# Last stage: first rounding of the convolution's result on GpSimd, ahead of its split of the recurrent state, instead of on ScalarE

## The reference, cut to what matters

```
# layer 1: LSTM over t, then a feed-forward with quantised activations
h = bit_linear(lstm_h, w1)          # act_quant(x): scale = 127 / max|x| per row,
h = depthwise_conv1d(h, conv_w, b)  #   clip(round(x * scale), -128, 127) / scale
h = silu(h)                         # 128 sequences x 512 channels for each step
x = x + bit_linear(h, w2)           # act_quant(h) again: this is the rounding moved here
# layer 2: h2 = tanh(h2 @ Wh + x @ Wx + b); x = x + W2 gelu(W1 h2 + b1) + b2
# layer 3: gate = sigmoid(h3 @ Wh.T + x @ Wz.T + b); h3 = tanh(h3 * leak + gate * x)
#          x = x + r * (relu(k) ** 2 @ W_v), r and k from two mixes of h3 and its predecessor
```

## Time and profile before

| | |
|---|---|
| time, median of 3 runs (lowest to highest) | 550.9 us (550.57 to 550.95) |
| the profiled execution: its own time | 550.28 us |
| its span, first to last instruction | 549.0 us |
| PE busy | 535.7 us, 98% of the span |
| DVE busy | 430.2 us, 78% |
| ACT busy | 380.4 us, 69% |
| POOL busy | 197.6 us, 36% |

### The profile page before, as it was taken

The page is one execution under the profiler, slowest core; times in us unless marked ns, Lnnn a source line. Parts: engine busy times, 40 slices in busy tenths (PEclk is TensorE's granted clock), DMA queues, the critical chain, the costliest instruction groups (busy, mean ns, idle before and its releaser), DMA issues.

```text
span 549.0 us, 10031 instructions
## 1 busy us (share of the span) xinstructions
PE 535.7 (98%) x3309; PEld 464.1 (85%) x3309; DVE 430.2 (78%) x1042; ACT 380.4 (69%) x857; POOL 197.6 (36%) x186
## 2 busy tenths in 40 slices
PE   8999999999999999999999989999999999999997
PEld 7877888887877899999999877789999999987785
DVE  4987655676868888668756259989999999999866
ACT  5567767768766755344553256988988888888965
POOL 4688788888788203939000000010000000000100
DMA  8634305521090302030000000111111111111211
GB/s 290 192 153 159 153 4 229 193 111 44 1 338 11 135 4 80 0 117 21 1 1 0 1 1 1 27 32 21 20 19 22 20 31 35 36 36 41 49 50 38
DMA packets 30226, 37.35 MB, mean 68 GB/s; under 512 B 20096, under 2 KB 23648, under 8 KB 29280
## 3 DMA queue, kind: packets, MB, share of 16 engines
q1 hardware_dynamic: 30176, 36.72, 20.8%
HBM read 30.24 MB, written 2.28 MB: 59 GB/s over the span
## 4 chain that ended last, share of the span: by engine, by line
PE 80%; DVE 13%; ACT 3%; issue 2%; POOL 2%; DVEq 0%; ACTq 0%
PE bank L325 10%; PE bank L1264 10%; PE bank L326 10%; PE bank L327 10%; PE bank L1689 4%; PE bank L1775 4%; PE bank L1679 4%; PE bank L1716 3%; PE bank L1717 3%; PE bank L1332 2%; PE bank L1214 1%; POOL hidden_low L387 1%; PE bank L1764 1%; PE bank L1802 1%; PE bank L1788 1%
## 5 line engine op out<-in xcount | busy, mean ns | idle before, releaser
L387 POOL TENSOR_TENSOR hidden_low<-hidden,hidden_high 128x512 fp32r<-128x512 f32 x72 | 94.5, 1320 | 21.5 <-ACT hidden_high L372 19.3
L2070 POOL CAST h_high<-h 128x256 fp32r<-128x256 f32 x15 | 6.4, 426 | 197.5 <-ACT h L1881 191.1
L468 ACT ACTIVATE bank<-bank 128x512 f32<-128x512 f32 x56 | 32.6, 583 | 30.4 <-PE bank L327 30.1
L472 DVE TENSOR_TENSOR hidden<-bank,big 128x512 f32<-128x512 f32 x56 | 38.5, 687 | 14.3 <-ACT bank L468 13.3
L372 ACT CAST hidden_high<-hidden 128x512 fp32r<-128x512 f32 x70 | 43.1, 615 | 4.4 <-DVE hidden L472 3.1
L325 PE MATMUL bank<-xin_high,sw_high 128*128 128x256 f32 x128 | 43.9, 343 | 0.0
L1716 PE MATMUL bank<-taps_high,q1T 128*128 128x512 f32 x94 | 42.8, 456 | 1.0 <-ACT q1T L1844 0.6
L1717 PE MATMUL bank<-taps_low,q1T 128*128 128x512 f32 x94 | 37.1, 395 | 0.0
L1817 ACT ACTIVATE gates_t<-bank,lstm_b_half 128x128 f32<-128x128 f32 x96 | 28.2, 364 | 12.1 <-PE bank L1689 8.8
L1398 DVE COPY yT<-bank 128x256 f32<-128x256 f32 x32 | 13.5, 423 | 28.9 <-PE bank L1264 28.9
L1679 PE MATMUL bank<-x,lstm_wx 128*128 128x128 f32 x256 | 34.4, 277 | 1.7 <-ACT gates_t L1817 0.9
(11 more groups left out here) (274 smaller groups left out, 1734.8 us busy)
## 6 DMA issues: line engine op xcount, KB each, us to landing
big<-gates_scratch SPq DMA_DIRECT2D x7, 2048.0 KB, 7.6
w<-in_f_w SPq DMA_DIRECT2D x16, 256.0 KB, 5.9
onehot<-topi_scratch SPq DMA_DIRECT2D x8, 512.0 KB, 4.0
outT<-x SPq DMA_DIRECT2D x15, 128.0 KB, 2.1
xT<-in_xT SPq DMA_DIRECT2D x3, 512.0 KB, 6.9
hidden<-in_ffn_w SPq DMA_DIRECT2D x3, 256.0 KB, 5.3
hidden<-in_conv_w SPq DMA_DIRECT2D x3, 256.0 KB, 4.4
xT<-in_xT SPq DMA_DIRECT2D x2, 256.0 KB, 4.0
```

Of the source, the lines that this page charges most:

```text
L387: pool.tensor_tensor(hidden_hl[u % 3][1][:, :], hidden[u % 3][:, :], hidden_hl[u % 3][0][:, :].bitcast(F32), ALU.subtract).then_inc(s_lo, 1)
L472: dve.tensor_tensor(hidden[u % 3][:, :].rearrange("p (i k) -> p i k", k=P), r_bank[j % 2][:, :].rearrange("p (i k) -> p i k", k=P), gate_r ...
```

## The change

`round_hs` leaves ACT's program at all its 32 places and becomes a POOL instruction of the same result, a tensor_scalar with a multiplication by the column sc2 and an addition of MAGIC. The waits are the same two (c_sc2 and, from the second pair on, c_q2), now on POOL. The diff, with the calls taken out of ACT's list cut to two places:

```diff
-            def round_hs(t):
-                if has(t):
-                    act.wait_ge(c_sc2, t // 2 + 1)
-                    if t >= 2:
-                        act.wait_ge(c_q2, t // 2)
-                    act.activation(v2[:, t % 2, :], hs[:, (t // 2) % 2, t % 2, :], ACT.Identity, bias=magic[:, 0:1],
-                                   scale=sc2[:, t:t + 1]).then_inc(c_v2, 1)
...
+            def round_hs(t):
+                if has(t):
+                    pool.wait_ge(c_sc2, t // 2 + 1)
+                    if t >= 2:
+                        pool.wait_ge(c_q2, t // 2)
+                    pool.tensor_scalar(v2[:, t % 2, :], hs[:, (t // 2) % 2, t % 2, :], sc2[:, t:t + 1], MAGIC,
+                                       ALU.mult, ALU.add).then_inc(c_v2, 1)
...
                 for q in range(FILL, TURNS):
                     tanh_rnn(2 * (q - 6) + 1)
                     tanh_cell(2 * (q - 1))
-                    round_hs(2 * (q - 4))
                     store_q1(q - 2)
-                    round_hs(2 * (q - 4) + 1)
                     tanh_state3(2 * (q - 8) + 1)
...
             def pool_program():
                 pool_init()
                 ready(pool)
-                for p in range(PAIRS):
-                    split_h2(p)
+                for t in range(6):
+                    round_hs(t)
+                split_h2(0)
+                round_hs(6)
+                round_hs(7)
+                split_h2(1)
+                for p in range(4, NPAIR):
+                    round_hs(2 * p)
+                    round_hs(2 * p + 1)
+                    split_h2(p - 2)
+                split_h2(NPAIR - 2)
```

More of the change, by code:

```diff
@@ L2344, in act_program @@
                 tanh_output(7)
-                round_hs(0)
-                round_hs(1)
                 tanh_cell(7)
@@ L2356, in act_program @@
                 scale_y(0)
-                round_hs(2)
                 tanh_gates(9)
-                round_hs(3)
                 tanh_output(9)
@@ L2373, in act_program @@
                 scale_y(2)
-                round_hs(4)
-                round_hs(5)
                 tanh_gates(11)
@@ L2388, in act_program @@
                 round_h(10)
-                round_hs(6)
                 round_h(11)
                 tanh_cell(12)
-                round_hs(7)
                 store_q1(5)
@@ L2440, in act_program @@
                 scale_y(26)
-                round_hs(28)
-                round_hs(29)
                 tanh_state3(21)
@@ L2455, in act_program @@
                 scale_y(28)
-                round_hs(30)
                 tanh_gate3(23)
-                round_hs(31)
                 quantise_hs(15)
```

## The result

Measured in turn on one chip, the changed kernel takes 552.8 us at the median of 6 runs (551.77 to 552.97), the kernel before 550.74 us (550.29 to 551.12). The ratio is 1.0033, with a 95% interval of 1.0021 to 1.0046: slower, by 2.1 us between the medians and 1.8 us by the ratio. The prediction was 553.2 us.

A forecast was written before the change was run, and what follows sets the result against it. PE bounds the loop; the tail's chain runs over VectorE, then PE. Terms 0.8 + 1.0 + 0.4 + 0.25 - 0.2 = +2.25 us gave 552.5 us for the profiled execution, 553.2 for the median; range 550.4 to 557.5.

The forecast's parts named there:

- Block 11, +0.8: Tail, pair 13: two roundings ahead of the split make L2072 late, so its reader on PE starts 0.8 us late.
- Block 12, +1.0: Tail, pair 14: roundings ahead of the split make its reader on PE start 1.0 us late, on PE's chain.
- Split 13 "has over 2 us to spare at its reader": Tail, behind pair 15: the split still comes over 2 us ahead of its reader, so no cost was counted.
- The loop, +0.4: Loop: roundings delay VectorE, so PE gets L1967's bank 0.04 to 0.15 us late in six turns, +0.4 taken.
- L2025 stands still for it: Loop: VectorE's L2025, with two SBUF inputs, is held while the first rounding runs to 419.66.
- The ramp, +0.25: Ramp, pair 0: second rounding meets L1936 near 343.2; if the rounding wins, VectorE is 0.5 us late, otherwise nothing.
- ScalarE's relief, -0.2: Ramp and tail: ScalarE reaches its next calls 0.8 us earlier a round, taken as -0.2 us.
- v2 is not late for `quantise_hs`: Rounding on GpSimd takes 692 ns, less than ScalarE's 807, so its result reaches `quantise_hs` in time.
- VectorE as the loop's bound: Rival, 11%: no rounding finds cover, VectorE needs 13.88 us a turn against PE's 13.35; 557.0 us.
- a slow rounding: Rival, 5%: a rounding takes 1.93 us as L246 does, making the tail's splits later; about 558 us.
- Faster: Rival, 14%: ScalarE's queue sets the tail, and pairs 14 and 15 each give back some 0.8 us; 549.3 us.
- No change: Rival, 14%: the tail's shifts are taken back later, or ScalarE's relief offsets the late splits; 551 us.

The follow-up runs named there:

- Number 6: Kernel before, all roundings on ScalarE, plus two 128x864 memsets on GpSimd into an unused buffer ahead of each of splits 11 to 13: 552.07 us, ratio 1.0029.
- numbers 4: Changed kernel with only pairs 13 to 15 rounded on GpSimd, the other pairs on ScalarE: 552.80 us, ratio 1.0032.
- Number 5: Kernel before, all roundings on ScalarE, plus two extra roundings on spare buffers on GpSimd ahead of each of splits 11 to 13: 553.07 us, ratio 1.0041.
- Number 2: Changed kernel with the two roundings of pair 15 back on ScalarE: 551.96 us, ratio 1.0020.
- numbers 3 and 9: Changed kernel with pairs 13 to 15 rounded on ScalarE again, run twice: 551.85 us, ratio 1.0015, and 551.53 us, ratio 1.0009.
- numbers 7 and 10: Changed kernel with pair 0 and pairs 13 to 15 rounded on ScalarE again, run twice: 550.32 us, ratio 0.9994, and 551.05 us, ratio 1.0008.

## Why the prediction was right, term by term

The forecast (slower, 552.0 to 554.5 us) held, and the mechanism that it trusted most is the one that the chip shows. Of the sum:

- **Block 11, +0.8**: measured +0.74. L1764 waits for L2072, at 500.24. Number 6 shows that lateness alone gives +0.70.
- **Block 12, +1.0**: measured +0.92. sc2 ended 0.35 us earlier against its neighbours, as worked out, and L2072 at 511.93. Number 6 gives +0.76 of it to lateness by 1.57 us of memsets; the roundings took 1.79 us, and that longer time is the likely rest, not shown.
- **Split 13 "has over 2 us to spare at its reader"**: this step failed, by +0.46 (+0.38 and +0.40 in numbers 4 and 5). The reader did have the time. I looked only for who waits for the split, not for whom the split and the roundings meet on their way: VectorE's `p`, `x` and `pre`, which PE's L1738 waits for. Number 2 takes it away, and number 6 shows that the split's new time can cost 0.27 of it without a rounding.
- **The loop, +0.4**: measured -0.06, and the step that failed is "L2025 stands still for it". VectorE's instructions ran back to back and kept their 0.28 us, and GpSimd waited. In exchange L2072 moved off L2030 (now 0.35 us, not 0.82), and VectorE was 0.34 us a turn less busy. PE hid both, and the turn stayed at 13.35 us.
- **The ramp, +0.25**: measured -0.08. The meeting at 343.2 went to the rounding, as in the worse case that I gave; it held L1928 to 0.70 us, and PE was 0.44 us late at 344 us by the ledger, near the 0.5 of that case. But 0.22 of it was made up by 350 us, and another 0.3 came back at 359 and 370 us, where I had nothing.
- **ScalarE's relief, -0.2**: nothing that shows. Number 5, without it, has the same three steps. That "v2 is not late for `quantise_hs`" held.

The five terms made 2.25 us, the trace 1.97: four errors of 0.2 to 0.5 us (split 13, loop, ramp, relief) nearly cancel, and that the sum comes so near is luck; the two terms that carry the forecast, 1.8 of the 2.25, are not. The median was 0.4 us below 553.2, of which 0.28 is the sum and 0.16 that the kernel before ran at 550.74 in the comparison and not at 550.9.

Of the rivals, VectorE as the loop's bound is out (12.16 us in a turn of 13.35), a slow rounding too (0.69 to 1.43 us). "Faster" lived on relief that number 5 shows to be worth nothing. "No change" was right about the loop and the ramp, wrong about the tail: what is lost there isn't given back by 550 us.

## What to carry to other kernels

When work is moved to an engine that looks idle, look for what that engine does just in time, and at every place where it stands ahead of such work: here 26 of the 32 moved instructions cost nothing by the ledger and 6 cost 2 us, because in the tail GpSimd's split went straight to a waiting PE and its reads held VectorE. Swapping the order did not help: at one pair the moved work was itself awaited, at the next it held VectorE on PE's chain. Leaving those six where they were took the three steps away, but not the whole loss: numbers 3 and 9 were still 1.0 and 0.8 us slower at the median, with the late transposition in their traces, and numbers 7 and 10 could not be told from the kernel before. And when an instruction moves in time, ask not only who waits for it but what it now runs beside.

## What the runs showed of the hardware

- GpSimd's tensor_scalar with a column and an immediate, 128x512 f32, took 0.69 us free, and up to 1.43 when VectorE had instructions with two inputs in SBUF back to back; a single one of VectorE's took 0.70 for 0.28, 0.81 for 0.35 or 0.83 for 0.47 us where GpSimd had come first.
- A memset on GpSimd (0.82 us for 128x864) left VectorE's `xr` at 0.48 us, which fits the Trainium skill's page "SBUF — State Buffer" ("Who interferes with whom"): a VectorE instruction with two SBUF inputs does not contend with a GpSimd instruction that only writes. L2003 is of another form, one input, a tensor_scalar of 128x2: it takes 0.16 us alone, took 0.51 beside a split, and 0.97 where a memset of 128x512 followed the split (number 5), ending 0.03 us after the memset.
- Pair 14's transposition by DMA, which lands in 3.0 us, took 4.0 to 4.8 in the eight profiles in which a 16 KB packet of an instruction queue ran beside it, and the store issued behind it then held SP's queue for up to 1.69 us instead of 0.57. None of the 128 transpositions without such a packet beside them took over 3.07 us.
